# Eight of 32 key tiles summed in half-precision parts, six score groups late, in a resonance-attention and FP4 kernel

## The reference

```python
x_norm = layernorm(x, gamma, beta)
q, k = l2_normalize(heads(x_norm @ w_q)), l2_normalize(heads(x_norm @ w_k))     # 16 heads of 16
v = heads(x @ w_v)
resonance = 0.5 + 0.5 * tanh((q @ k.T - 0.27) * 15.0)                          # T x T, = sigmoid(30 (q.k - 0.27))
gate_q, gate_k = (0.25 + 0.75 * sigmoid(a @ g) for a, g in ((q, g_q), (k, g_k)))
fused = (resonance * gate_q[..., :, None] * gate_k[..., None, :]) @ v
x = layernorm(x + fused @ w_o + b_o)
x = layernorm(x + fp4_ffn(x))     # gate, up: 256 -> 704; silu(gate) * up; down: 704 -> 256; all operands rounded to FP4
```

## Time and profile before

| | |
|---|---|
| time, median of 2 runs | 4403.53 us |
| the profiled execution | 4404.2 us, its span 4402.4 us |
| PE busy | 4119.8 us (94%) |
| ACT busy | 4021.6 us (91%) |
| DVE busy | 1562.0 us (35%) |
| POOL busy | 159.4 us (4%) |
| chain that ended last | PE 68%, ACT 16%, issue 8%, DVE 4%, DMA 2% |
| granted TensorE clock | 0.993 of 2.4 GHz, mean of the span |

### The profile page before, as it was taken

One profiled execution on the slowest core, in us unless ns is written; L12 is line 12 of the kernel. 1 busy time (PEld: TensorE's weight loads), 2 busy tenths in 40 slices (PEclk: granted clock), 3 DMA queues, 4 the chain that ended last, 5 costly groups with the idle time before them and its releaser, 6 DMA issues.

```text
span 4402.4 us, 80654 instructions
## 1 busy us (share of the span) xinstructions
PE 4119.8 (94%) x28776; PEld 1290.5 (29%) x28776; DVE 1562.0 (35%) x4540; ACT 4021.6 (91%) x3271; POOL 159.4 (4%) x120
## 2 busy tenths in 40 slices
PE   7988899999999999999999999999999999999997
PEld 5651222222222222222222222222222222222223
DVE  6754023323332333333233323333333333333236
ACT  4669999999999999999999999999999999999993
POOL 2330000000000000000000000000000000000001
PEclk9999999999999999999999999999999999999998
DMA  3454443344434433444344434443344334433440
GB/s 109 127 127 78 70 76 58 60 77 77 61 60 73 78 62 62 70 78 65 62 68 77 71 56 68 77 71 61 63 77 72 60 62 77 77 58 60 77 82 13
DMA packets 179953, 314.46 MB, mean 71 GB/s; under 512 B 65264, under 2 KB 141808, under 8 KB 154608
## 3 DMA queue, kind: packets, MB, share of 16 engines
q1 hardware_dynamic: 179568, 309.41, 41.5%
HBM read 266.82 MB, written 42.47 MB: 70 GB/s over the span
## 4 chain that ended last, share of the span: by engine, by line
PE 68%; ACT 16%; issue 8%; DVE 4%; DMA 2%; SPq 2%; POOL 0%; ACTq 0%; POOLq 0%; DVEq 0%
PE ps L1269 34%; PE ps L1259 19%; ACT room L698 15%; PE ps L1296 8%; PE ps L1319 4%; DMA m_f<-fused_t 2%; DVE room L850 1%; SPq L523 1%; SPq L499 1%; PE ps L1214 0%; PE ps L1281 0%; DVE st L804 0%; DVE xnT L840 0%; PE ps L1225 0%; PE ps L1206 0%
## 5 line engine op out<-in xcount | busy, mean ns | idle before, releaser
L698 ACT ACTIVATE room<-ps 128x1024 f32<-128x1024 f32 (+1 forms) x2816 | 3790.7, 1415 | 183.1 <-PE ps L1259 167.3
L1269 PE MATMUL ps<-room,vt 128*32 128x512 f32 x16384 | 2052.8, 602 | 0.0
L1259 PE MATMUL ps<-qs,room 64*128 64x512 f16 x8198 | 1325.9, 383 | 213.8 <-ACT room L698 192.6
L1259 PEld LDWEIGHTS ps<-qs,room 64*128 64x128 f16 x8198 | 310.8, 93 | 1758.3 <-ACT room L698 1107.0
L1269 PEld LDWEIGHTS ps<-room,vt 128*32 128x32 f32 x16384 | 388.4, 108 | 947.0 <-issue 947.0
L1296 PE MATMUL ps<-wguT,m_xqT 128*128 128x352 f32 x960 | 348.2, 485 | 0.0
L959 DVE TENSOR_TENSOR vz<-ps,vz 128x352 f32<-128x352 f32 x120 | 63.0, 525 | 757.7 <-ACT vz L708 757.7
L964 DVE TENSOR_TENSOR vz<-ps,vz 128x352 f32<-128x352 f32 x120 | 63.0, 525 | 595.8 <-PE ps L1296 595.8
L1319 PE MATMUL ps<-wdnT,wqk 128*128 128x256 f32 x720 | 198.9, 404 | 0.6 <-DVE wqk L929 0.6
L1296 PEld LDWEIGHTS ps<-wguT,m_xqT 128*128 128x128 f32 x960 | 162.6, 189 | 105.1 <-issue 54.3
L592 POOL TENSOR_TENSOR m_x<-m_x,bo 128x256 f32<-128x256 f32 x60 | 43.8, 730 | 3890.9 <-DMA m_x<-in_L_attn_x_dram 3890.9
(11 more groups left out here) (172 smaller groups left out, 2206.4 us busy)
## 6 DMA issues: line engine op xcount, KB each, us to landing
room<-k_parts SPq DMA_DIRECT2D x520, 256.0 KB, 9.2
vt<-v_gated SPq DMA_DIRECT2D x65, 1024.0 KB, 17.5
qs<-q_parts SPq DMA_DIRECT2D x520, 32.0 KB, 10.0
gqb<-q_gates SPq DMA_DIRECT2D x256, 64.0 KB, 2.1
room<-in_L_attn_x_dram SPq DMA_DIRECT2D x16, 512.0 KB, 4.2
v_gated<-vz SPq DMA_DIRECT2D x64, 128.0 KB, 2.1
fused_t<-fs SPq DMA_DIRECT2D x256, 32.0 KB, 1.6
q_parts<-room SPq DMA_DIRECT2D x30, 256.0 KB, 2.8
```

The lines of the kernel that those rows point to most:

```text
L698: act.activation(res[:, c, o:o + m, :], ps[:, o:o + m, :], ACT.Sigmoid, scale=2 * SHARP / QK_UP ** 2, bias=-2 * SHARP * THRESH).then_inc(b ...
L1259: ins = pe.matmul(ps[:, BANK[n % 2] + i, :], ks[o:o + HROWS, par, h // 2, kt * P:(kt + 1) * P], qs[o:o + HROWS, par, h // 2, :], start=Tru ...
L1269: ins = pe.matmul(ps[32 * h:32 * h + 32, SUM_BANK, :], vt[:, par, n * HD:n * HD + 32], r, start=kt == 0, stop=kt == KT - 1, skip_group_che ...
```

## The change

The sums of eight key tiles of a unit, 3c for c = 0, 1, 2, 4, 5, 6, 7, 8 (`SPLIT`), are no longer made in single precision in step 4c but in half precision in step 4c + 6, in all units from the fifth on (`j >= 1`).

- DVE makes two half-precision parts of the four sigmoid tiles of group 4c: a scaled high part (`r_hi`) and the rest (`r_lo`), each 128 x 2048 (`split_results`). Its calls are strung between the pieces of the feed-forward work, whose functions are cut up for it.
- POOL scales the values of the next unit by a power of two (`scale_values`, 128 x 2048 and 128 x 128), and makes their high and low parts for the eight tiles (six instructions more). The scale is found at the end of stage A from the largest value, for which DVE reduces each step's values in stage A (`vmx`).
- PE multiplies both parts of the values at once (16 columns each of a strip of 32) with first `r_hi` and then `r_lo` (`split_sums`): eight half-precision matmuls per key tile where there were four of single precision. Step 4c + 6 waits for the DVE parts (`b_cv`) before its scores. The other key tiles' stationary operand is 16 columns wide instead of 32. Key tile 1 now comes first and also waits for POOL (`b_v`).
- Each head's strip holds two partial results. Both are stored, so `store_sums` issues eight DMAs, `load_sums` is called twice (`m_f`, `m_f2`), and POOL adds the two before piece P, which waits for `l_fs` instead of `l_f`. The last stage adds the two by four more matmuls per tile instead. `load_unit` has one load more.

The diff, cut to its core:

```diff
-        at[4 * c + 2] = [0, 1] if c == 0 else [3 * c + 1]
+        at[4 * c + 2] = [1, 0] if c == 0 else [3 * c + 1]
     return at.get(g, [])
+def split_at(n):
+    return [SPLIT.index(c) for c in SPLIT if 4 * c + 6 == n]
+SPLIT = [0, 1, 2, 4, 5, 6, 7, 8]
+NST = 2 * HG
...
# SyncE
+                sp.dma_start(vp[:, par, :, 0:HD], vd[b, g, :, FIRST_KT, :].rearrange("p (h d) -> p h d", d=HD))\
                   .then_inc(b_in[par], 16)
...
                 for h in range(HG):
-                    sp.dma_start(fd[b, (g * HG + h) * HD:(g * HG + h + 1) * HD, bass.ds(i * BLK, BLK)],
-                                 fs[32 * h:32 * h + HD, :]).then_inc(b_st, 16)
+                    for lo in range(2):
+                        o = 32 * h + lo * HD
+                        sp.dma_start(fd[b, lo, (g * HG + h) * HD:(g * HG + h + 1) * HD, bass.ds(i * BLK, BLK)],
+                                     fs[o:o + HD, :]).then_inc(b_st, 16)
...
-                    load_sums(m_f[:, :, :], j - 1, g).then_inc(l_f, 16)
+                    load_sums(m_f[:, :, :], 0, j - 1, g).then_inc(l_f, 16)
+                    load_sums(m_f2, 1, j - 1, g).then_inc(l_f, 16)
...
# GpSimd, in each unit, after m_x + bias
+                    pool.wait_ge(l_f, 32 * (k + 1))
+                    pool.tensor_tensor(m_f[:, :, :], m_f[:, :, :], m_f2, ALU.add).then_inc(l_fs, 1)
+            def scale_values(j, g):
+                pool.wait_ge(b_in[par], 16 * NIN * (2 * j + g // 2 + 1))
+                ins = pool.tensor_scalar(vt[:, par], vt[:, par], v_up, None, ALU.mult)
+                ins = pool.tensor_scalar(vp[:, par], vp[:, par], v_up, None, ALU.mult)
...
+                for v, hi, lo in parts:
+                    ins = pool.tensor_scalar(v, v, 1 / RES_UP, None, ALU.mult)
...
+                    ins = pool.tensor_copy(hi, v)
...
+                    ins = pool.tensor_tensor(lo, v, hi, ALU.subtract)
+                ins.then_inc(b_v, 1)
...
# VectorE, stage A, in each step
+                    after(dve.tensor_reduce(vmx[:, TB:2 * TB], vz[:, par, :, 0:D], AX_X, ALU.max,
+                                            apply_absolute_value=True))
+                    after(dve.tensor_tensor(vmx[:, 0:TB], vmx[:, 0:TB], vmx[:, TB:2 * TB], ALU.max))
...
# VectorE, stage B
+            def split_results(u, g, i):
+                n = 4 * SPLIT[i]
+                r = res[:, (NGRP // 2 * g + n // 2) % RES_CYCS, 0:HG, :].rearrange("p h n -> p (h n)")
+                if i >= 2:
+                    dve.wait_ge(b_pv, u * KT + SPLIT_POS[i - 2] + 1)
+                dve.wait_ge(b_act, u * NGRP + n + 1)
+                after(dve.tensor_scalar(r_hi[i % 2], r, RES_UP, None, ALU.mult))
+                dve.scalar_tensor_tensor(out=r_lo[i % 2], in0=r, scalar=RES_UP, in1=r_hi[i % 2],
+                                         op0=ALU.mult, op1=ALU.subtract).then_inc(b_cv, 1)
...
+                    split_results(u, g, 0)
+                    if ends(j, g):
+                        end_transposes(k - 1, (1,))
+                    split_results(u, g, 1)
+                    begin_tile(k, par)
+                    split_results(u, g, 2)
+                    begin_quantize(k, par)
+                    if ends(j, g):
+                        end_tile(k - 1, 1 - par)
+                    split_results(u, g, 3)
+                    turned(k)
+                    split_results(u, g, 4)
+                    for p in range(4):
+                        gates(k, (p,))
+                        if p < 3:
+                            split_results(u, g, 5 + p)
+                    hidden(k)
...
# TensorE
+            def split_sums(i, par):
+                for part in (r_hi[i % 2], r_lo[i % 2]):
+                    for h in range(HG):
+                        ins = pe.matmul(ps[32 * h:32 * h + 32, SUM_BANK, :], vh[:, par, i, 32 * h:32 * h + 32],
+                                        part[:, h * BLK:(h + 1) * BLK], start=False, stop=False, skip_group_check=True)
+                ins.then_inc(b_pv, 1)
...
-                    pe.wait_ge(l_f, 16 * (k + 1))
+                    pe.wait_ge(l_fs, k + 1)
...
+                    for i in split_at(n):
+                        if split:
+                            pe.wait_ge(b_cv, (u - HG) * NSPLIT + i + 1)
                     if n + 2 < NGRP:
                         scores(n + 2, par)
...
-                        sums(kt, par, g)
+                        if not (split and is_split(kt)):
+                            sums(kt, par, g)
+                    for i in split_at(n):
+                        if split:
+                            split_sums(i, par)
```

More of the change, by code:

```diff
@@ L919, in to_grid, with end_transposes @@
                 return dve.tensor_tensor(dst.rearrange("p (n e) -> p n e", e=16), t3, bcast(scale, 16), ALU.mult)
-            def end_transposes(k):
-                for half in range(2):
+            def end_transposes(k, halves=(0, 1)):
+                for half in halves:
                     dve.wait_ge(l_H, 2 * k + half + 1)
@@ L1381, in unit @@
                         turn_weights(PREP[n])
+            pe.wait_ge(a_ev, TB * NBLK)
+            pe.wait_ge(v_mxd, 1)
+            pe.transpose(ps[0:1, C_BANK, 0:P], v_mx, idf[:, :]).then_inc(v_row, 1)
+            pe.wait_ge(b_ev, 1)
+            pe.wait_ge(v_oned, 1)
+            pe.matmul(ps[:, C_BANK, P:P + 1], ones, v_one, start=True, stop=True).then_inc(v_col, 1)
             pe.wait_ge(a_evA, 3 * (NBLK - 1))
```

158 lines of the change are left out of this document (126 added, 32 removed).

## The result

The changed kernel takes 4814.18 us (4805.97 and 4822.40 in two runs), against 4403.53: ratio 1.0935, 95% interval 1.0907 to 1.0963. The forecast was 4620, the range ended at 4720. The direction was right, the size was missed by half: +410 us instead of +216.

A forecast was written before the change was run, and what follows sets the result against it. ACT sets a floor of 59.7 us a unit; saved PE work is worth at most 2.7. Sum: 4404.2 + 180 (units) + 22 (stage A) + 9 (start of stage B) + 5 (end) = 4620 us; range 4495 to 4720.

The forecast's parts named there:

- order on PE and pairs: Steps around the pieces: split sums move PE's work ahead of them; 3.5 us of ACT waits a unit without P.
- rival A: Piece P, step 7: P is not late, loads overlap or land sooner; unit 63.6 us, +75, total 4515; chance 0.17.
- P late: Piece P, step 7: more stores, second load and POOL's add delay it; ACT waits 2.2 us before group 10.
- 0.05 from the end of scores to ACT: Handoff from PE's scores to ACT, taken as 0.05 us in stepping through the unit.
- the walk: Step-by-step timing of a unit's 44 steps on PE and ACT; forecast 65.4 us a unit against 62.4.
- The clock: PE's clock in the unit: granted in full, no PE idle piece over 2 us, so a lower level got no chance.
- Rival C: Pairs 4 to 7 beside `scale_values`: DVE and POOL hold each other up; 2 us a unit, total 4740; chance 0.08.
- POOL: Hidden: `scale_values` (at most about 4.08 us) and six small instructions, 6 to 10 us, finish before the next unit's step 2.
- So all of it counts: Stage A: DVE's reduction and maximum, 1.4 us in the chain of each of 16 steps, +22 us.
- B: DVE pair 3, for step 22, comes late as the high part takes 2.29 us; +30 to 45 us; chance 0.09.
- D: Steps 4c + 2 before a piece: PE's total, not order, holds ACT back; 2.7 us a unit gained, 4278; chance 0.05.
- E: P not late and waits behind pieces stay near before, split sums overlapping; unit 62.4 to 63.2, 4440 to 4490; chance 0.11.

The follow-up runs named there:

- e3_neither: Changed kernel without POOL's scaling and part instructions and without the low strip's stores, second load and add (work left out to measure its time): 4576.1 us.
- e2_no_low: Changed kernel without the low strip's way through memory: four stores, one `m_f` load, no POOL add, low sums missing from the result: 4653.9 us.
- e1_no_pool: Changed kernel without POOL's scaling of the 128 x 2048 values and its six part instructions; P as late as before: 4739.2 us.
- e7_no_max: Changed kernel without the reduction and maximum of the values in each step of stage A, scale from a constant 1: 4756.5 us.
- e4b_before_moved: Kernel before, only its order changed: key tile 3c summed in step 4c + 2 instead of step 4c: 4748.3 us, +349.
- e11_three: Changed kernel with constant scale, three split rounds over 16 rows, no low strip, early `m_x` load, new key-tile order: 4343.3 us, ratio 0.9872 to the kernel before.

## Why the prediction was right or wrong

Term by term, in us over the run:

| term | forecast | measured | from |
|---|---|---|---|
| order on PE and pairs | 72 (63.6 a unit, rival A) | 132 | 60 intervals of e3_neither, 3885.0 - 3752.9 |
| P late | 108 | 167 | changed - e2_no_low, 4127.1 - 3960.5 |
| DVE against POOL | 0 | 79 | changed - e1_no_pool, 4127.1 - 4048.5 |
| up to the first `fs` | 31 | 43 | 428.4 - 385.2 |
| end | 5 | 1 | 84.4 - 83.2 |

The measured column gives 422 where 418 are missing (4822.4 - 4404.2, the profiled executions); the two causes were taken away one at a time, and single runs differ by some 30 us in the intervals.

In short: half of the loss was forecast by the right mechanism. The other half stood in three terms: the waits after the pieces were sized too small, P's lateness was taken as one value with no fall of the clock behind it, and DVE against POOL was left at nothing.

**Right.** The mechanism of the quiet unit: PE's work falls, but the split sums stand behind a key tile and ahead of a piece, and P waits for POOL's sum. The split sums cost 0.42 (0.43), the high part 1.22 (1.23), the low part 2.29 (2.29), four more stores with SP's wait 1.95 (2.08), and the waits of ACT came where they were forecast. The waits before groups 5, 7, 11, 19 and 35 are gone.

**The order, +60.** "0.05 from the end of scores to ACT" was too little. With 0.12 and 0.11 at each handoff, as the trace of the changed kernel shows where ACT has waited, the walk gives 64.3 without the late P; 64.63 were measured, and these last 0.3 us stay unexplained. The error is small in each wait: in e3_neither ACT waits 0.51 before group 10, 0.94 before 14 and 0.83 before 34 and 38 (forecast 0.4, 0.77, 0.68, 0.68), and 0.29 before each of the two gate sigmoids, where 0.09 stood; the waits before 15, 18 and 39 came out no longer than forecast. One sum of the prediction is also off: the waits it lists without P add up to 4.0 us, not 3.5. The walk, on which the forecast rests, is not touched by it.

**P late, +59.** What failed is that one value stood for all units, and that no price was set on the clock behind it. For the quiet unit the value was right: 66.05 - 64.63 = 1.4 us where the forecast had 1.8. In e1_no_pool, where P is late and POOL's large instruction is gone, the 32 units at full clock last 66.35 us, 1.7 more than those of e3_neither; the 28 others last 68.76, 4.1 more. There PE waits 2.9 us before P in the mean instead of 1.8, and the rest comes with the lower clock. The spread was there to be read in the kernel before: its `m_f` is issued 4.2 to 6.5 us after the first store, and the prediction took it from one unit; the landing of 5.7 us in the earlier trace rows was worked out as a bound, with 5 us of wait, but went neither into the sum nor into the range. And "The clock: ... I give a lower level no chance of its own" was wrong. It followed from "PE has no idle piece over 2 us there by the walk", and PE had one before P in 32 of 60 units.

**DVE against POOL, +79.** Rival C had the mechanism, its place and about its size (120), and 0.08 for a chance. What it stood on, "halved to 2 us it would just fit", was a price for POOL's scaling between 2 and 4.08 us. Measured: 5.44 alone. The one-input instruction is dearer than the two-input row of the same width (whose output is half precision), so the bound from above did not hold. POOL's other work was underpriced as well: with the scaling, and without its two adds, it is busy 17.7 us in the quiet unit, where the terms of the forecast give 14 at most. "POOL: Hidden" was right of the result (POOL never came late with it) and wrong of the instruction beside it.

**Stage A and the start, +12.** "So all of it counts" was right of the direction; what was missing is 1.64 us a step instead of 1.4, and PE's lower clock in most steps. That the reduction brings that lower clock is shown by e7_no_max, where it is 1.00 again; by what way stays open. The scaling at the start took 6.0 us with its small one instead of 3.4.

**Rivals.** A: the wait at P is real. B: the high part is 1.22 us, so it does not apply. D is refuted by e4b_before_moved. E: the waits did not overlap away.

## What to carry to other kernels

Where two engines are both nearly full and only one piece of work deep ahead of each other, the place of the work counts more than its amount: nine key tiles moved by two steps cost 5.8 us of 62, and eight tiles made cheaper by half were worth something only after the rest was set out anew and P was on time. Work out such an order with the prices of the work it is for (e11_three lost 23 us in units with other prices), and recheck handoffs in a trace where the waiting engine really waits. A new link in a chain that already had little slack should be priced over the spread of all units and not from one, since here a pause on PE cost twice, once as a wait and once through the clock behind it.
